# ScalarE's work on x moved between steps, GpSimd's statistics in five parts, and the last two batches' mixing on TensorE

## What is computed

```python
x = x + jnp.tanh(g_xattn[0]) * _L0_xattn_ref(_layernorm(x, axis=-1), ctx_4096, mask, ...)   # windows of 128
# _L0_ffn_ref of _layernorm(x):
x_norm = x * jax.lax.rsqrt(jnp.mean(x * x, axis=-1, keepdims=True) + RMS_EPS)
H_res = sinkhorn_log(x_norm @ W_res.T ... + H_res_base)     # 50 iterations on 4 x 4 per row
H_pre = jax.nn.softmax(x_norm @ W_pre.T + H_pre_base); H_post = ...   # 4 numbers per row
x_pre = jnp.einsum('btnc,btn->btc', x_streams, H_pre)       # the mixing: 4 streams to one
y = x_pre @ W_branch                                        # 512 x 512
x_mixed = jnp.einsum('btij,btjc->btic', H_res, x_streams)
return (x_mixed + jnp.einsum('btc,btn->btnc', y, H_post)).reshape(B, T, nC)
```

## Time and profile before

| | us |
|---|---|
| median of 3 runs (1815.07 to 1822.41) | 1816.63 |
| the profiled execution | 1819.56 |
| its span, first to last instruction | 1817.4 |
| DVE busy | 1337.7 (74%) |
| PE busy | 1348.6 (74%) |
| ACT busy | 1130.6 (62%) |
| POOL busy | 818.0 (45%) |

### The profile page before, as it was taken

The page is one execution under the profiler, slowest core; times in us unless marked ns, Lnnn a source line. Parts: engine busy times, 40 slices in busy tenths (PEclk is TensorE's granted clock), DMA queues, the critical chain, the costliest instruction groups (busy, mean ns, idle before and its releaser), DMA issues.

```text
span 1817.4 us, 35773 instructions
## 1 busy us (share of the span) xinstructions
PE 1348.6 (74%) x12292; PEld 839.2 (46%) x12448; DVE 1337.7 (74%) x3566; ACT 1130.6 (62%) x2273; POOL 818.0 (45%) x1373
## 2 busy tenths in 40 slices
PE   2679999988788888887988788888888876512223
PEld 0446566555455555554555455555555553301011
DVE  3334433666579877988798878987798878779987
ACT  3457777777677757776677757775777765311111
POOL 3224335354646563656455655657365634420000
PEclk9789999999999989999999989999999997755556
DMA  8457676666566766776677657775667553321122
GB/s 253 134 144 206 186 190 185 176 173 188 166 173 192 199 186 187 198 203 176 187 201 196 174 152 200 199 198 156 176 181 181 144 135 105 93 81 58 58 99 109
DMA packets 175460, 299.89 MB, mean 165 GB/s; under 512 B 25105, under 2 KB 76177, under 8 KB 171185
## 3 DMA queue, kind: packets, MB, share of 16 engines
q1 hardware_dynamic: 157872, 264.04, 48.1%
q0 software_dynamic: 17408, 33.56, 10.6%
HBM read 179.81 MB, written 67.11 MB: 136 GB/s over the span
## 4 chain that ended last, share of the span: by engine, by line
DVE 34%; PE 18%; ACT 16%; issue 15%; POOL 14%; SPq 2%; DMA 2%; POOLq 0%; ACTq 0%; DVEq 0%
PE pr L660 7%; POOL kp L561 6%; DVE ssum L1212 6%; DVE otile_even L1241 4%; ACT squares L923 3%; DVE xpre L1229 3%; DVE otile_odd L1241 3%; DVE sa L1213 3%; DVE negm L1090 2%; PE pr L674 2%; DVE sv L1213 2%; ACT xt L915 2%; POOL x1c L503 2%; DVE otile_even L1257 2%; ACT probs L883 2%
## 5 line engine op out<-in xcount | busy, mean ns | idle before, releaser
L1212 DVE TENSOR_REDUCE ssum<-kp 128x16 f32<-128x64 f32 x768 | 181.3, 236 | 123.6 <-POOL kp L561 119.2
L561 POOL TENSOR_TENSOR kp<-ke,sa 128x64 f32<-128x64 f32 x343 | 152.7, 445 | 247.5 <-DVE sa L1213 247.5
L561 POOL TENSOR_TENSOR kp<-ke,sv 128x64 f32<-128x64 f32 x329 | 149.1, 453 | 199.8 <-DVE sv L1213 199.1
L774 PE MATMUL av_ps<-probs,v_t 128*32 128x128 f32 x2048 | 111.3, 287 | 153.8 <-DVE o_sb L1098 151.0
L660 PE MATMUL pr<-x_hl,wq 128*128 128x512 bf16 x707 | 180.7, 403 | 43.3 <-POOL x_hl L484 36.0
L883 ACT ACTIVATE probs<-st_ps,key_bias 128x512 f32<-128x512 f32 x256 | 173.0, 676 | 63.0 <-PE st_ps L761 62.9
L1098 DVE TENSOR_TENSOR o_sb<-av_ps,rden 128x128 f32<-128x128 f32 x256 | 72.9, 285 | 177.9 <-ACT rden L892 173.8
L1090 DVE TENSOR_REDUCE negm<-s_ps 128x4 bf16<-128x512 f32 x256 | 166.2, 649 | 49.8 <-PE s_ps L747 49.6
L484 POOL TENSOR_TENSOR x_hl<-xc,x_hl 128x512 bf16<-128x512 f32 x128 | 151.5, 1183 | 106.0 <-ACT x_hl L851 106.0
L674 PE MATMUL pr<-wv,ctx_hl 128*128 128x256 bf16 x1536 | 182.3, 276 | 21.0 <-DVE k_hl L1075 17.9
L687 PE MATMUL pr<-o_sb,wo 128*128 128x512 bf16 x705 | 181.7, 385 | 12.2 <-DVE x1c L1108 5.0
(11 more groups left out here) (149 smaller groups left out, 3066.7 us busy)
## 6 DMA issues: line engine op xcount, KB each, us to landing
xs<-in_dram SPq DMA_DIRECT2D x128, 256.0 KB, 5.7
xc<-in_dram SPq DMA_DIRECT2D x128, 256.0 KB, 4.0
ctx_raw<-in_dram SPq DMA_DIRECT2D x32, 1024.0 KB, 7.6
x1c<-in_dram POOLq DMA_DIRECT2D x64, 512.0 KB, 7.5
x_dram<-x1c SPq DMA_DIRECT2D x32, 1024.0 KB, 4.2
q_st<-q_hl SPq DMA_DIRECT2D x384, 64.0 KB
k_st<-k_hl SPq DMA_DIRECT2D x384, 64.0 KB
x1t_even<-x_dram SPq DMA_DIRECT2D x16, 1024.0 KB, 6.5
```

What stands on the lines that cost most here:

```text
L561: nc.gpsimd.tensor_tensor(kp[:], ke[:], v, ALU.mult).then_inc(kp_made, 1)
L774: nc.tensor.matmul(av_ps[rows, 0:W], v_t[:, G % 2, w, et * P + h * DH:et * P + (h + 1) * DH], probs[:, k % 2, h * W:(h + 1) * W], start=Tr ...
L1212: cf.link(nc.vector.tensor_reduce(s_t, k, AX.X, ALU.add))
```

## The change

ACT normalises tiles 0 and 1 of x at r = 0 and 1 instead of 1 and 4, POOL splits them at r = 1 and 3 instead of 3 and 5; one of the squares moves from r = 3 to r = 4. POOL's first half of `add_x` (r = 7) moves from ahead of part 2 to ahead of part 3. The statistics are issued as `moments` in two parts (u = 13), `scale_b` in two parts (u = 14) and `norm_b` (u = 16), half of them ahead of part 3; `variance` and `xstat` come one step earlier. For batches 6 and 7 the mixing of the four streams leaves DVE: ACT makes five diagonal matrices of 128 x 128 (`diagonals`; they lie in `ctx_raw`, which is free by then), and PE multiplies blocks of `x1t` by them (`mix_pre`), which gives the mixed tile transposed at once; `transpose_pre` goes for these tiles.

```diff
-HI_X_AT, LOW_X_AT = [1, 4, 5, 6], [3, 5, 6, 7]
+HI_X_AT, LOW_X_AT = [0, 1, 5, 6], [1, 3, 6, 7]
-SQUARES_AT = [3, 3, 4, 4]
+SQUARES_AT = [3, 4, 4, 4]
-BEHIND = dict(load=-5, first=-3, xpre=-3, pre=-2, branch_0=-1, branch_1=-1, out_0=-1, out_1=0,
+BEHIND = dict(load=-5, diag=-3, mix=-2, branch_0=-1, branch_1=-1, out_0=-1, out_1=0,
...
@@ POOL's loop
-                if 0 <= G - 1 < NG and r == 7:
-                    add_x(G - 1, 0)
                 if 0 <= G - 2 < NG and r == 0:
                     add_x(G - 2, 1)
                 if g >= 0 and u == 15 and b + 1 < B:
-                    variance(b + 1)
-                if g >= 0 and u == 16 and b + 1 < B:
                     xstat(b + 1)
-                for part in range(3):
-                    for ready in ffn_at(g, STAT_AT + 1 + part):
-                        stat_b(ready, part)
+                for ready in ffn_at(g, STAT_AT + 1):
+                    moments(ready, 0)
+                for ready in ffn_at(g, STAT_AT + 2):
+                    scale_b(ready, 0)
                 scale_at(f, its, 2)
...
+                if 0 <= G - 1 < NG and r == 7:
+                    add_x(G - 1, 0)
                 for H, t in at_step(g, -2, LOW_X_AT):
                     split_x(H, t)
+                for ready in ffn_at(g, STAT_AT + 1):
+                    moments(ready, 1)
+                for ready in ffn_at(g, STAT_AT + 2):
+                    scale_b(ready, 1)
+                for ready in ffn_at(g, STAT_AT + 4):
+                    norm_b(ready)
                 scale_at(f, its, 3)
+                if g >= 0 and u == 14 and b + 1 < B:
+                    variance(b + 1)
@@ PE
+            def mix_pre(what, part):
...
+                if part == 0:
+                    pe.wait_ge(x1t_loaded[n % 2], 16 * (n // 2 + 1))
+                    pe.wait_ge(diag_made, n - DT * (LAST_BESIDE + 1) + 1)
+                for j in (2 * part, 2 * part + 1):
+                    block = bank(what)[:, j * P:(j + 1) * P]
+                    for i in range(N):
+                        at = i * C + j * P
+                        nc.tensor.matmul(block, x1t[n % 2][:, at:at + P], diag[:, n % 2, i, :], start=(i == 0),
+                                         stop=False)
+                    ins = nc.tensor.matmul(block, ones[:], diag[:, n % 2, N, :], start=False, stop=True)
@@ ACT
+            def diagonals(f, t):
...
+                for i in range(N):
+                    nc.scalar.activation(diag[:, n % 2, i, :], id_sb[:], ACT.Identity, scale=pre[:, f % 3, t, i:i + 1])
+                nc.scalar.activation(diag[:, n % 2, N, :], id_sb[:], ACT.Identity, scale=rb[:, f % 3, 6, t:t + 1]
+                                     ).then_inc(diag_made, 1)
...
-                if g >= 0 and u == 15 and b + 1 < B:
+                if g >= 0 and u == 14 and b + 1 < B:
                     xstat(b + 1)
```

More of the change, by code:

```diff
@@ L104, in tiles_at @@
     return [(f, t) for (f, t), at in TILE_AT.items()
-            if g == at + (BESIDE if f <= LAST_BESIDE else BEHIND)[part]]
+            if g == at + (BESIDE if f <= LAST_BESIDE else BEHIND).get(part, LAST)]
 def sink_at(g):
@@ L133, in banked_at @@
     made = [("sel", f, 0) for f in ffn_at(g, UPC + SELECT_AT)]
+    made += [("mix", f, t) for f, t in tiles_at(g, "mix")]
+    assert len(made) < 2
     if 0 <= G + 1 < NG:
@@ L524, in xstat, with moments @@
                 nc.gpsimd.tensor_scalar(ra[:, 4, :], ra[:, 4, :], -1.0, None, ALU.mult).then_inc(xstat_ready, 1)
-            def stat_b(f, part):
+            def moments(f, part):
                 r = rb[:, f % 3]
@@ L542, in stat_b, with scale_b @@
                     nc.gpsimd.tensor_scalar(r[:, 0, :], r[:, 8, :], LN_EPS, None, ALU.add).then_inc(rs_req, 1)
-                elif part == 1:
+            def scale_b(f, part):
+                r = rb[:, f % 3]
+                if part == 0:
                     pool.wait_ge(rs_req, 2 * f + 1)
@@ L550, in stat_b, with norm_b @@
                     nc.gpsimd.tensor_scalar(r[:, 4, :], r[:, 4, :], RMS_EPS, None, ALU.add).then_inc(rs_req, 1)
[L551 to L555, removed]
+            def norm_b(f):
+                r = rb[:, f % 3]
+                pool.wait_ge(rs_req, 2 * f + 2)
+                pool.wait_ge(rs_done, 4 * f + 4)
+                newton(r[:, 5, :], r[:, 2, :], r[:, 4, :], r[:, 1, :])
+                nc.gpsimd.tensor_tensor(r[:, 5, :], r[:, 5, :], r[:, 3, :], ALU.mult).then_inc(rb_ready, 1)
             def scale(f, it, half):
@@ L735, in transpose_pre @@
                 ins.then_inc(bank_full, 1)
+            def mix_pre(what, part):
+                kind, f, t = what
+                n = DT * f + t
+                if part == 0:
+                    pe.wait_ge(x1t_loaded[n % 2], 16 * (n // 2 + 1))
[7 more added lines that the diff above has]
+                    ins = nc.tensor.matmul(block, ones[:], diag[:, n % 2, N, :], start=False, stop=True)
+                if part:
+                    ins.then_inc(bank_full, 1)
             def scores(k):
@@ L800, in _ @@
                 for n, what in enumerate(made):
-                    if what[0] != "sel":
+                    if what[0] not in ("sel", "mix"):
                         bank_free(what)
@@ L814, in _ @@
                         select(what, 1)
+                    elif what[0] == "mix":
+                        mix_pre(what, 1)
                     elif what[0] == "pre":
@@ L826, in _ @@
                         branch(f, t, part)
-                for f in ffn_at(g, UPC + SELECT_AT - 1):
-                    bank_free(("sel", f, 0))
-                    select(("sel", f, 0), 0)
+                for what in banked_at(g + 1):
+                    if what[0] == "sel":
+                        bank_free(what)
+                        select(what, 0)
+                    elif what[0] == "mix":
+                        bank_free(what)
+                        mix_pre(what, 0)
         @block.scalar
@@ L974, in first_out @@
                 n = DT * f + t
+                if pair == 0:
+                    act.wait_ge(x1t_loaded[n % 2], 16 * (n // 2 + 1))
                 if t == 0 and pair == 0:
@@ L1015, in _ @@
                     first_products(done, t)
+                for done, t in tiles_at(g, "diag"):
+                    diagonals(done, t)
                 for pair in range(2):
@@ L1034, in _ @@
                         copy_lg(what)
-                    elif what[0] == "pre":
+                    elif what[0] in ("pre", "mix"):
                         copy_pre(what)
```

13 lines of the change are left out of this document (12 added, 1 removed).

## The result

The changed kernel took 1840.3 us (median of 4 runs, 1834.56 to 1845.67) against 1817.16 of the kernel before: a ratio of 1.0122, 95% interval [1.0077, 1.0167]. It is slower by 22 to 23 us. The forecast was 1808, range 1795 to 1823, with 0.13 for slower.

The account below looks back on a forecast made before the run. It took PE and ACT to bound without the sinkhorn, DVE and POOL's ring beside it, DVE in the last stages. Main loop +11.3 and tail -20.2 gave -8.9 us, from 1816.63 to 1808, range 1795 to 1823.

Parts of the forecast that it names:

- the first bullet: Main loop, r = 7: DMA issue moved behind part 2 delays POOL's `kp`, +0.8 us a chunk, bounds 0 and +1.2.
- The sum of a chunk: Main loop, chunks with sinkhorn and output together: POOL's new places add +1.8 us each, +18 for ten.
- r = 3: Main loop: POOL's split goes from here to r = 1; POOL had holes, 0 us, bounds -0.3 and +0.3.
- ACT's relief: Main loop: ACT earlier, -3 us in six chunks without sinkhorn and -3 at u = 19 to 22.
- r = 1: Main loop: POOL's split beside `xpre` and DVE's third L1229 delays `kp`, +0.6 us a chunk, bounds 0 and +1.1.
- u = 16: Main loop, statistics: the sum's stall of 1.89 us goes whole, `norm_b` then lying behind part 2, -1.9 us.
- u = 13: Main loop, statistics: four of the chain's nine links go behind part 2, 1.0 of the 2.15 us wait goes.
- u = 18: Main loop: POOL's added work beside the logits blocks one more operation for 1.0 us, 4 batches, +4.
- r = 5: Main loop: split gone, but three squares in a row on ACT make `rden` late, +0.3 us, bounds -0.5 and +0.35.
- The tail: Last stages: -10.7 us from L1229 leaving DVE, -1.5 statistics, -8 last three tiles; -20.2, bounds -26 and -5.
- rival C: Last stage: PE's clock stays low and PE becomes the bound, +6 in place of -8; 1822 us, chance 0.17.
- Rival D: Main loop: POOL wins the port each time, main loop +24, net +4; 1821 us, chance 0.11.

Follow-up runs that it names:

- the last run: One square moved from r = 3 to r = 4, nothing else, against the kernel with mixing and statistics (1791.1 us): 1797.06 us, ratio 0.9891.

## Why the prediction was wrong

The step that failed is the first bullet, "r = 7, the DMA issue behind part 2: +0.8". It reckoned the serial time of POOL and left DVE's stream as it was. The run with the split first has that cost, +0.73. In the order of the change the stream, begun beside the issue, stood through the whole split as well, and 0.8 became 1.23, beyond the upper bound of 1.2. The places were counted right, 18 of them. But the fifteen with output cost 1.22 to 1.26 each, and the three without, in which DVE has no stream beside POOL and the serial time shows whole, 1.45 to 1.47. That makes 22.9 us where the term had 15 (8.3 + 2.4 + 4.2): 8 of the 19 us by which the main loop was missed. Why the three cost more than the issue's own 1.2, which is what they cost with the split first, is open.

The rest is in other terms. The sum of a chunk, +1.8, was one of +0.8, +0.6 and +0.3, which is 1.7. r = 3 was put at 0 and has +5.2. r = 4 and r = 5 came out at 0.0 together, where ACT's relief of -6 stood.

- Not in the sum at all: what a longer r = 7 and the new tables do together to the steps r = 3 to 5. In the medians the DMA cost 26.7 us without the tables (1817.8 against 1791.1) and 41.8 with them (1840.3 against 1798.5), so some 15 us are theirs together; the changed kernel's four times lie in two pairs 9 us apart, so this figure is a loose one. The main loops of the traces differ by as much (38.7 us against 23.4), and r = 3, 4 and 5 have all of it. Some 11 us are in two kinds of place: six slow V projections behind the start, against two with the DMA put back, and six steps u = 3 and 27 behind one at the low clock, against two. That speaks for the place at which the clock falls, and not for how often. It is argued and not shown: the run with new tables for x and old squares had nine slow V projections and five such steps, and its main loop took 1436.9 us, as long as with the DMA put back (1437.7). No run held the clock fixed.
- r = 1: +0.6 forecast, 0.45 measured. u = 16: -1.9 forecast, -1.93 measured. u = 13: -1.0 forecast, -1.34 in the changed trace, one chunk of the four before being slow; against the three others it is -1.05. But only half of that is the statistics': with them and the old tables a chunk at the full clock took 7.02 against 7.52, and the wait of the sum fell by 0.5 (2.15 to 1.65); the other 0.55 came with the tables of x. u = 18: +1.0 forecast, +0.41 against the kernel before, whose own four u = 18 spread from 8.46 to 10.02 us; against mixing and statistics (8.70 to 8.82) the run with the tables too has 9.65 to 9.78, the +1.0 of the forecast.
- r = 5: +0.3 forecast, +1.5; but r = 4 gave 1.1 to 1.5 in the same chunks, which the forecast had at 0. The square in this pair is worth +0.7 by the last run. Beside the sinkhorn ACT's relief, -3 in the forecast, gave nothing that the pair of r = 4 and 5 kept; without the sinkhorn the chunks fell from 37.4 to 36.9 us, the 0.5 forecast.
- The start, +3.5 us: not looked at. It goes with the tables (75.3 to 78.8 us in the eight experiments with the old tables for x, 79.6 to 83.2 in the changed kernel and the four experiments with the new). In the chain that ended last SP's row of DMAs into `q_st` and `k_st`, 0.6 us each, begins at 51.07 us in place of 48.25: ACT has another tile to normalise ahead of the copy that the first of them waits for.
- The tail: -20.2 forecast, -18.7 measured, -18.0 with the mixing alone. By its parts the last tiles gave more (11.3, 15.5 and 11.2 us against 13.8 forecast), the part beside the sinkhorn less: batch 7's half iterations on DVE took 113.7 us (1661.4 to 1775.1) against 122.2, -8.5 where -12.2 stood. The granted clock of the last stage rose from 0.64 to 0.81, y from 6.76 to 3.70 us. So rival C, in which it stays low, fell, and the Trainium skill's rule (TensorE: Matmul & The Clock Gate, Part 1) is borne out by the two rows. The sum of the tail is close because the misses of its two parts offset each other, which is luck.
- Rival D had the right side, the port, at the wrong place: it expected it at r = 1 (+1.1, measured +0.45) and u = 18 (+2).

The statistics (-10.2 alone) and the mixing (-15.6 alone) are near the forecast, -11.3 and about -19. What turned the change is the DMA (+28 alone) and the tables (+7 or +36, by what stands beside them).

## What to carry to other kernels

Where two engines exclude each other, an operation's price can be that of what the other engine has queued next as well as of what it is doing: work out who is on the way when it begins, and try the order within the gap, which here was worth 13 us without moving anything out of it. A moved consumer must be checked against the step in which its producer runs, in every step of the period: `xstat` and the normalising in r = 0 met in one step of 32, and making `xstat` earlier gave 13.5 us back. And parts of one change should be timed apart and in pairs, since two of them added up (-25 us), two were worse together by some 15 us, and one cost 36 us alone and 7 behind another.
